# A new order of projections in an attention and FFN kernel: queries and keys first, values last, and the layernorm of the projected rows five units later

## The reference

```
x = x + layernorm(attention(layernorm(x)))     # 32 heads of 16, causal, rotary tables on q and k
x = x + layernorm(ffn(layernorm(x)))           # silu(x gate^T) * (x up^T), down^T, inner size 1408
attention: q, k, v = x W^T + b; q, k = rope(q), rope(k); softmax(q k^T / 4, causal) v; then W_o and b_o
```

## Time and profile before

| | |
|---|---|
| three runs | 3097.47, 3098.64, 3099.94 us |
| the profiled execution, its time | 3105.56 us |
| its span, first to last instruction | 3103.8 us |
| TensorE busy | 2601.8 us (84%) |
| VectorE busy | 2199.6 us (71%) |
| ScalarE busy | 1330.8 us (43%) |
| GpSimd busy | 1020.0 us (33%) |
| exponentials (L525) | 640, from 96.2 to 2041.9 us |
| mean granted TensorE clock | 0.943 of full speed |

### The profile page before, as it was taken

One profiled execution on the slowest core, in us unless ns is written; L12 is line 12 of the kernel. 1 busy time (PEld: TensorE's weight loads), 2 busy tenths in 40 slices (PEclk: granted clock), 3 DMA queues, 4 the chain that ended last, 5 costly groups with the idle time before them and its releaser, 6 DMA issues. The chain is left out here.

```text
span 3103.8 us, 59189 instructions
## 1 busy us (share of the span) xinstructions
PE 2601.8 (84%) x19584; PEld 1260.9 (41%) x19584; DVE 2199.6 (71%) x6495; ACT 1330.8 (43%) x1710; POOL 1020.0 (33%) x1051
## 2 busy tenths in 40 slices
PE   3788878788778888888887888853999999999997
PEld 1343434444334344444344444321444444444443
DVE  4878879788778797887788877836555545545544
ACT  2455555555545555555455555524222222222222
POOL 3454455454544554545446545310000000000000
PEclk9899999999999899998999989976999999999999
DMA  3222332322322323223223232222111111111111
GB/s 138 84 78 86 86 89 65 110 89 65 106 92 80 94 63 108 90 63 112 90 75 98 64 100 76 73 88 87 41 54 41 68 42 53 68 41 54 68 41 41
DMA packets 94356, 237.07 MB, mean 76 GB/s; under 512 B 13456, under 2 KB 63888, under 8 KB 80912
## 3 DMA queue, kind: packets, MB, share of 16 engines
q1 hardware_dynamic: 94096, 233.64, 23.7%
HBM read 148.39 MB, written 84.15 MB: 75 GB/s over the span
## 5 line engine op out<-in xcount | busy, mean ns | idle before, releaser
L673 DVE CUSTOM_DVE_ANT_0 mx<-mx,causal 128x512 f32<-128x512 f32 (+3 forms) x2048 | 944.2, 517 | 267.6 <-PE mx L798 265.4
L525 ACT ACTIVATE probs<-ts,exp_scale 128x1024 f32<-128x1024 f32 x640 | 712.7, 1114 | 723.3 <-PE ts L812 723.2
L451 POOL TENSOR_SCALAR_AFFINE_SELECT probs<-probs 128x512 f32<-128x512 f32 x512 | 321.0, 644 | 774.7 <-ACT probs L525 774.7
L1218 DVE SCALAR_TENSOR_TENSOR hidden<-gu,up_scale,silu 128x512 f32<-128x512 f32 x176 | 131.9, 750 | 417.4 <-PE gu L1268 407.7
L798 PE MATMUL mx<-kT,qT 64*128 64x512 f16 (+3 forms) x2048 | 263.3, 315 | 181.3 <-DMA kT<-slots 89.6
L1077 ACT ACTIVATE silu<-gu,gate_scale 128x512 f32<-128x512 f32 x176 | 120.9, 687 | 631.1 <-PE gu L1268 631.1
L1052 POOL TENSOR_TENSOR f_rstd<-f_var,f_neg_half 128x4 f32<-128x4 f32 x32 | 32.3, 1009 | 928.5 <-DVE f_var L1195 647.5
L812 PE MATMUL ts<-qT,kT 64*128 64x512 f16 (+3 forms) x2048 | 258.1, 310 | 71.0 <-DMA qT<-shift_rows 57.6
L826 PE MATMUL xb<-probs,vs 128*32 128x512 f32 (+3 forms) x4096 | 312.1, 446 | 1.0 <-POOL probs L451 1.0
L1266 PE MATMUL gu<-f_xT_hi,gate_hi 128*128 128x512 f16 x704 | 267.7, 380 | 52.2 <-issue 52.2
L673 DVE DVE_READ_ACCUMULATOR2_ANT row_max<- 128x1 f32 x2048 | 283.6, 138 | 0.0
(11 more groups left out here) (145 smaller groups left out, 4597.8 us busy)
## 6 DMA issues: line engine op xcount, KB each, us to landing
slots<-half_hi SPq DMA_DIRECT2D x512, 64.0 KB
qT<-slots SPq DMA_DIRECT2D x128, 256.0 KB, 3.9
kT<-slots SPq DMA_DIRECT2D x128, 256.0 KB, 3.9
xn<-x SPq DMA_DIRECT2D x16, 1024.0 KB, 4.9
xr<-x SPq DMA_DIRECT2D x16, 1024.0 KB, 5.6
slots<-half_lo SPq DMA_DIRECT2D x256, 64.0 KB
x<-xr SPq DMA_DIRECT2D x16, 1024.0 KB, 5.6
f_xn<-x SPq DMA_DIRECT2D x16, 1024.0 KB, 4.7
```

Of the source, the lines that this page charges most:

```text
L451: nc.gpsimd.affine_select(out=d, in_=d, compare_op=ALU.is_ge, fill=0.0, base=0, pattern=[[0, HG], [1, P]], channel_multiplier=-1).then_inc ...
L525: nc.scalar.activation(probs[:, g % 2, u, :, :], ts[:, :, :], ACT.Exp, scale=exp_scale[:, 0:1]).then_inc(ts_read, 1)
L673: last = nc.vector.tensor_tensor_reduce(out=scores, in0=scores, in1=causal[:, T - P * (qt + 1):T], scale=1.0, scalar=-3e38, op0=ALU.add, o ...
```

## The change

The order of the tiles, the units of the layernorm of the projected rows, the unit of one transposition and of two transfers, and the form of one wait.

```
-                     (("out", 3, -1), ("q", 0, 1)), (("k", 0, 1), ("v", 0, 1)), (("q", 1, 1), ("k", 1, 1)),
-                     (("v", 1, 1), ("q", 2, 1)), (("k", 2, 1), ("v", 2, 1)))
+                     (("q", 0, 1), ("k", 0, 1)), (("out", 3, -1), ("q", 1, 1)), (("k", 1, 1), ("q", 2, 1)),
+                     (("k", 2, 1), ("v", 0, 1)), (("v", 1, 1), ("v", 2, 1)))
...
-                         19: ("a", 0, 0), 29: ("a", 1, 0), 39: ("a", 2, 0)}
+                         24: ("a", 0, 0), 29: ("a", 1, 0), 39: ("a", 2, 0)}
...
-        STATISTICS1_AT = {11: 0, 13: 1, 16: 2, 18: 3}
-        VARIANCE1_AT = 19
-        NORMALISE1_AT = {21: (0, 1), 22: (2,), 23: (3,)}
-        RESIDUAL_AT = {22: (0, 1), 23: (2,), 24: (3,)}
+        STATISTICS1_AT = {11: 0, 13: 1, 16: 2, 23: 3}
+        VARIANCE1_AT = 24
+        NORMALISE1_AT = {26: (0, 1), 27: (2,), 28: (3,)}
+        RESIDUAL_AT = {27: (0, 1), 28: (2,), 29: (3,)}
...
-                    if s == 26 and exists(i - 1):
+                    if s == 31 and exists(i - 1):
...
-                    if s == 28 and exists(i - 1) and exists(i):
+                    if s == 33 and exists(i - 1) and exists(i):
...
-                    if kind == "q" and n == 0:
-                        pe.wait_ge(xT_ready, NC * (i + owner + 1))
...
+                        if kind == "q" and n == 0:
+                            pe.wait_ge(xT_ready, NC * (i + owner) + c + 1)
```

## The result

The changed kernel takes 3186.04 us (median of four runs, 3182.02 to 3189.56) against 3099.29 us of the kernel before, a ratio of 1.0263 with a 95% interval of 1.0242 to 1.0284. The forecast was slower, by 0.4%; it is slower by 2.6%, and outside the range of 3082 to 3134 us.

A forecast was written before the change was run, and what follows sets the result against it. SyncE's queue chain of low half, sends, fetches, store and shift was taken to bound unit 30; 65.6 + 39.6 + 18.6 = 123.8 us against 123.15, +10 us over 14 passes, +2 first pass: 3110 us, range 3082 to 3134.

The forecast's parts named there:

- main step: Both waits of unit 30 go (5.15 + 1.59 us); the same pattern returns five units later, at unit 35.
- 6.7 or a little more: Expected wait of `ts` at unit 35, about what `mx` and `ts` of unit 30 waited before, in us.
- I expect some 1.5 us there ... both are hidden, since VectorE is a unit behind. If that cover fails it costs up to 1.5.: At unit 25, `ts` waits some 1.5 us for q0's low half and a shift, hidden beside a wait for a0's low half.
- unit 24 to 35: Part two: old unit 19 to 30 (39.00 us) moved, plus 0.6 us for k0's low half on VectorE: 39.6 us.
- That ties with 18.5; I take 18.6.: Unit 35 to 0: chain of q2, k2, shift of group 0 ties with the 18.5 us low-clock path; 18.6 us taken.
- rival 3: Second chain takes 19.3 us, not 17.7, and unit 25's wait is uncovered: up to 1.6 + 1.5 us a sequence, 3125 to 3150; chance 0.15.
- Unit 0 to 24: Part one of a sequence: 48.40 us for unit 0 to 17 plus the units after, 65.6 us.
- the wait of unit 5: `ts` of unit 5 no longer waits 1.41 us for a shift, but TensorE waits longer at unit 9: worth nothing, at most 1.41.
- The start: First pass: shift of group 0 behind four sends, not two; between -4 and +13 us, +2 taken.

The follow-up runs named there:

- old tail: Changed kernel with the last three groups in the old order (k1 and v0, v1 and q2, k2 and v2); 3145.09 us.
- store behind the shift: Changed kernel with the store moved from unit 31 to 32, behind the shift of group 7, and the load of xr from 33 to 38; 3128.50 us.
- shift first: Changed kernel with each shift placed on SyncE in unit 1 of a group, ahead of that unit's fetch, not in unit 2; 3108.68 us.
- Late layernorm alone: Kernel before with statistics to residual sums in units 23 to 29, store in 31 and load in 33, tile order unchanged; 3077.52 us.
- load alone late: Changed kernel with only the load of xr moved to unit 38, the store staying in unit 31; 3157.34 us.
- store and load late: Changed kernel with shifts in unit 1 ahead of the fetch, the store in unit 32 and the load of xr in 38; 3037.44 us.

## Why the prediction was wrong in size

**The direction and its main step held.** The wait for kT at unit 30 is gone, and the stall is at unit 35 behind the shift of group 7. In passes 2 to 13 it is 6.9 to 8.5 us in the changed kernel and in its variant with the old tail, where 6.7 or a little more was reckoned. The 6.7 came from one sequence; over passes 2 to 13 of the kernel before, the two waits of unit 30 sum to 7.9 us on average, and after the change the wait at unit 35 is 7.9 us. The stall moved whole. With the store behind the shift it is 5.3 to 5.9 us and with shift first 2.1 to 2.8, so the store is one link of that chain, and the shift's place behind the fetches costs more. Late layernorm alone shows that moving the normalising, the store and the load away from q0's chain is worth 0.8%.

**"I expect some 1.5 us there ... both are hidden, since VectorE is a unit behind. If that cover fails it costs up to 1.5."** This is the first step that failed, and it carries 2.1 to 2.3 us of the 2.8 us missed from unit 24 to 35. The wait was 3.66 us in the sequence shown and 3.1 on average. Its length was taken from q3's chain, whose low half does not stand beside a GpSimd sine product; q0's took 1.07 us more, and its chain from send to `ts` 11.5 us for 10.5. Over 3 us the cover was no longer there: q1's send came 22.5 us after the exponential of unit 24 (956.38 - 933.91), 21.7 on average, and not 19.6, and the whole chain of unit 35 moved with it. The rest of the 2.8 is that chain itself, 20.8 us on average from q1's send to the exponential of unit 35 for 20.0 reckoned; the kernel before has 20.2 for its like. The granted clock in the 6 us behind unit 25 was 0.72, which the forecast had not counted either:

```profile
940.00:946.00 6.00, 6.00 (x30) 1.91 (x30) 2.46 (x7) 2.69 (x3) 3.15 (x3) 0.72 0.34 91
```

**"That ties with 18.5; I take 18.6."** The second failed step: 20.6 us. The chain of q2 and k2 was taken from units 39 to 5, where no 1 MB load runs beside it, plus 0.4. From q2's send to `ts` it took 20.4 us and not 17.7 to 18.1. The two fetches of that chain in the kernel before (its sends begin at 949.86):

```profile
955.31 1.16 SPq L359 DMA_DIRECT2D qT<-slots  x2
...
962.38 1.14 SPq L359 DMA_DIRECT2D kT<-slots  x2
```

From q2's send to its fetch it was 5.5 us there (955.31 - 949.86) and is 6.7 now (983.59 - 976.89), and k2's two fetch issues took 3.01 us for 1.14. Moving the load gave 1.8 us back, taking q2 and k2 out of that place 3.1. This was rival 3, which had 0.15 and was priced at 1.6 + 1.5 us a sequence; the two terms measured 2.0 and 2.8, and its upper end of 3150 us was 36 us too low.

**Unit 0 to 24** was 0.7 us longer than the sum. The part before had been read from one sequence with 53.90 us for units 0 to 19; the mean over twelve is 54.6. The changed kernel has 54.7 there, so the wait of unit 5 was worth nothing, as said; the wait of unit 9 grew from 0.6 to 1.1 us.

**The start** cost 6.1 us (first exponential of unit 0 at 102.4 for 96.2), with +2 taken and 13 as its bound. The shift of group 0 goes out at 97.9 us for 91.5. With the old tail, which takes q2 and k2 from ahead of it, it goes out at 86.4 and the exponential is at 93.6.

**Pass 0** stood nowhere in the sum, which counts 14 passes from 1 on. It took 119.0 us for 112.7, and 4.2 of these 6.3 us lie between units 35 and 0, where q2 and k2 stand in this pass too.

**The account**, from the two profiled executions: start 6.1, pass 0 6.3, passes 1 to 14 together 74.1 (14 times 5.3) where 10 were reckoned, from the last unit 0 to the end -6.6. That makes 79.9 us; the medians differ by 86.7. The -6.6, about 4 us in the attention phase and 3 behind it, was not looked into.

## What to carry to other kernels

A queue in which one engine issues everything in order turns each item's wait into the wait of all behind it. Before tiles are reordered, list for every consumer the last item that it needs and what stands ahead of it in that queue; an earlier producer helps only if it does not push another consumer's item back. Here the 8 KB of a shift (four transfers of 2 KB) were urgent and the 512 KB of a fetched tile were not. Putting the shifts first, in the time in which the queue waited for landings anyway, took 77 us off the changed kernel and 0.8% off the kernel before; the best order of tiles was worth 1.2% (2992 us for 3030 and 3032) once the queue was in order.

A stall that is expected to be hidden needs its length from a place with the same neighbours, and the length of its cover beside it. Where two bounds of a stretch tie, the one taken from another place is to be bounded from above, and a mean over several sequences is a surer base than one.

## What the runs showed of the hardware

- A VectorE product with two inputs in SBUF that began beside GpSimd's sine product took 1.75 us for 0.68 (above). Which of two VectorE instructions was hit changed with their order. Beside GpSimd's root of 4 columns the same instruction lost nothing.
- A wait's name can be that of another transfer. The jump between passes costs TensorE 3.4 to 4.6 us in the kernel before (passes 1 to 12) and up to 5.7 us in other runs; it is named "issue" in some kernels and "DMA kT<-slots" in others with the same code at that place, where a later fetch raised the same semaphore.
- k2's second fetch issue took 1.1 to 2.5 us in 9 of passes 1 to 13 of the changed kernel, where 0.56 is the median of all such issues. In the shift-first run q2's fetch did (2.68 us for two). With the load alone late no fetch issue of k took over 0.61 us, with store and load late six took over 1 us. The cause is open.
